# Six row buffers and loads five blocks ahead in the expert blocks of a two-layer recurrent kernel on one Trainium2 core

## The reference, cut to what matters

```python
residual = x
xn = _layernorm(x, ln_g, ln_b)
abel = jax.nn.gelu(xn @ aw1 + ab1, approximate=False) @ aw2 + ab2
nonabel = _rotate(_moe(xn, gate_w, gate_b, ew1, eb1, ew2, eb2), gens)
gate = jax.nn.sigmoid(jnp.concatenate([abel, nonabel], axis=-1) @ gc_w + gc_b)
return residual + abel * (1.0 - gate) + nonabel * gate
```

## Time and profile before

| what | us |
|---|---|
| median of three runs | 700.93 |
| lowest and highest of them | 700.16, 703.9 |
| the profiled execution | 701.6 |
| its span, from first to last instruction | 699.9 |

### The profile page before, as it was taken

How to read it: one execution, slowest core, us unless ns; L and a number is a source line. 1 busy time by engine, 2 the same in 40 slices (tenths; PEclk the granted TensorE clock), 3 DMA queues, 4 the chain that set the end, 5 groups by cost and what they waited for, 6 DMA issues and landing times.

```text
span 699.9 us, 19558 instructions
## 1 busy us (share of the span) xinstructions
PE 628.5 (90%) x6221; PEld 443.3 (63%) x6222; DVE 494.0 (71%) x1302; ACT 414.1 (59%) x1144; POOL 445.4 (64%) x652
## 2 busy tenths in 40 slices
PE   4788988886988898998899999998999999999993
PEld 3667767676877775775354455456999855555442
DVE  5678785568667716999488888885444488887884
ACT  2565433443444455776566777875444377878793
POOL 7675888889048889992122487843333258878782
PEclk9999999999999999997799999999999999999997
DMA  9995111144677731110000011100222201111110
GB/s 243 264 321 159 41 43 58 42 111 110 96 114 136 137 64 35 32 32 5 1 32 1 13 32 32 39 22 24 67 68 71 57 22 43 33 32 32 32 47 16
DMA packets 69466, 48.34 MB, mean 69 GB/s; under 512 B 8011, under 2 KB 63750, under 8 KB 69382
## 3 DMA queue, kind: packets, MB, share of 16 engines
q1 hardware_dynamic: 62332, 34.09, 19.3%
q0 software_dynamic: 6144, 12.63, 7.6%
q10 hardware_dynamic: 906, 0.55, 0.3%
HBM read 24.00 MB, written 23.24 MB: 67 GB/s over the span
## 4 chain that ended last, share of the span: by engine, by line
PE 49%; DVE 15%; POOL 13%; issue 9%; ACT 6%; DMA 5%; SPq 0%; DVEq 0%; POOLq 0%; ACTq 0%
PE bank L1753 12%; PE bank L1012 6%; PE bank L1733 6%; PE bank L1824 5%; PE bank L1833 5%; POOL yg_first L1056 4%; ACT pb L1898 3%; DVE nmx L2065 3%; DMA xg<-x_half 3%; POOL spacer L1051 3%; PE bank L579 2%; DMA y_half<-ys 1%; DVE turns L1392 1%; PE bank L1116 1%; POOL pool_xy L365 1%
## 5 line engine op out<-in xcount | busy, mean ns | idle before, releaser
L1898 ACT ACTIVATE pb<-bank,nmx 128x512 f32<-128x512 f32 x256 | 173.6, 692 | 64.7 <-DVE nmx L2065 64.5
L2065 DVE TENSOR_REDUCE nmx<-bank 128x2 f32<-128x1024 f32 x128 | 155.2, 1216 | 15.2 <-PE bank L1753 14.4
L1230 ACT ACTIVATE turns<-bank,cols 128x128 f32<-128x128 f32 x148 | 46.4, 364 | 57.1 <-PE bank L1116 56.3
L1665 POOL TENSOR_TENSOR vs<-vt_first,rz 128x256 f32<-128x256 f32 x64 | 39.5, 617 | 61.5 <-DVE rz L2041 60.8
L1733 PEld LDWEIGHTS bank<-pb,vs 128*32 128x32 f32 x2048 | 54.1, 110 | 37.4 <-issue 22.2
L1733 PE MATMUL bank<-pb,vs 128*32 128x128 f32 x2048 | 68.9, 275 | 2.0 <-POOL vs L1665 2.0
L382 POOL DMA_INDIRECT x_half<-pool_xy,slot x64 | 62.6, 977 | 10.6 <-issue 10.6
L1753 PE MATMUL bank<-qk 64*128 64x512 f32 x256 | 65.6, 622 | 1.6 <-ACT pb L1898 1.5
L1753 PE MATMUL bank<-qk_first 64*128 64x512 f32 x256 | 65.8, 632 | 1.2 <-ACT qk_first L1282 0.7
L1665 POOL TENSOR_TENSOR vs<-vt,rz 128x256 f32<-128x256 f32 x64 | 39.3, 617 | 39.0 <-DVE rz L2041 34.8
L1698 POOL COPY xn_all<-w 128x512 f32 x39 | 24.0, 616 | 47.6 <-PE bank L1824 47.6
(11 more groups left out here) (275 smaller groups left out, 1444.7 us busy)
## 6 DMA issues: line engine op xcount, KB each, us to landing
y_half<-ys SPq DMA_DIRECT2D x74, 64.5 KB, 2.7
x_half<-zero SPq DMA_DIRECT2D x2, 2368.0 KB, 17.1
xg<-x_half SPq DMA_DIRECT2D x74, 64.0 KB
x_sorted<-zero SPq DMA_DIRECT2D x1, 2496.0 KB, 18.7
xn_all<-x_sorted SPq DMA_DIRECT2D x39, 64.0 KB, 1.8
y_sorted<-xn_all SPq DMA_DIRECT2D x39, 64.0 KB, 1.6
x_all<-in_L_attn_x_dram SPq DMA_DIRECT2D x8, 256.0 KB, 6.3
w<-in_L_ffn_W_dram SPq DMA_DIRECT2D x1, 2048.0 KB, 11.3
```

The source lines that it names most:

```text
L1665: pool.tensor_tensor(vs[s][:, :, :], vt[bt % 2][:, n // 2 % TT, :, :].rearrange("p j d -> p (j d)") .unsqueeze(1).broadcast_to([P, 2, D]), ...
L1898: act.activation(pb[s + ab][:, :], psum[score_banks(k) + ab], ACT.Exp, bias=nmx[:, s + ab:s + ab + 1], scale=1.0, accum_out=zz[:, s + ab:s ...
L2065: dve.tensor_reduce(nmx[:, s:s + 2], banks[:, score_banks(k):score_banks(k) + 2, :], AX.X, ALU.max, negate=True).then_inc(n_mx, 1)
```

## The change

There are six row buffers in place of four; the two new ones are `cmask` and `bv_bc`. A load thus waits for the transposition of the block six earlier, and in step i SyncE issues the load of block i+5, still ahead of the store of block i-3. The load of block 4, the first into `cmask`, waits for the end of the first attention. SyncE no longer waits for stores; VectorE waits for the store of the block six earlier in `finish_block`, from block 6 on. Two semaphores go: `f_w`, which nothing used, and `f_og`, whose two waits count on `f_gg` instead.

```diff
-        NXG = 4
-        xg0 = [sbe(f"xg0{i}", [P, D]) for i in range(NXG)]
+        NXG = 6
+        xg0 = [sbe(f"xg0{i}", [P, D]) for i in range(NXG - 2)] + [cmask, bv_bc]
...
-        f_w = sem("f_w")
...
-        f_og = sem("f_og")
...
-                act.activation(og[:, :], gt[:, :], ACT.Copy, bias=0.5, scale=-0.5).then_inc(f_og, 1)
+                act.activation(og[:, :], gt[:, :], ACT.Copy, bias=0.5, scale=-0.5).then_inc(f_gg, 1)
...
-                act.wait_ge(f_og, bt + 1)
+                act.wait_ge(f_gg, 2 * bt + 1)
...
-                if k >= NB0 - LEAD:
+                if k >= NY:
                     dve.wait_ge(o_st[k % NY], 16 * (k // NY))
...
-                dve.wait_ge(f_gg, bt + 1)
+                dve.wait_ge(f_gg, 2 * bt + 2)
...
+                if k == NXG - 2:
+                    sp.wait_ge(a_os, B * TT + 2)
                 if k >= NXG:
                     sp.wait_ge(o_T, k - NXG + 1)
-                if k >= NY + LEAD:
-                    sp.wait_ge(o_st[(k - LEAD) % NY], 16 * ((k - LEAD) // NY))
```

## The result

The changed kernel takes 700.26 us (median of 20 runs, 697.58 to 702.55). The kernel before, run beside it, takes 702.43 us (20 runs, 699.68 to 706.06). The ratio is 0.9963, with a 95% interval of 0.9949 to 0.9978: 2.6 us faster (1.5 to 3.6), where the two medians differ by 2.2 us. The forecast was a gain of 4.4 us, or 0.63%. The sign is right and the size is too large; at 0.37% the change lies within the 0.5% that was counted as no change.

What follows compares the result with a forecast made beforehand. The prediction took the expert stage's first half, paced by late row loads, to bound the kernel. Loads five ahead gave 4.4 us and the other parts nothing: 700.93 - 4.4 = 696.5 us, range 693.2 to 700.3.

Steps and rivals of the forecast that it cites:

- The loads bound the pace: Expert stage, first half: late row loads, 3.88 us against three blocks of lead, set the pace, measured at 1.333 us a block.
- first item: Loads five blocks ahead: the pace over 29 first-half blocks falls from 1.333 to 1.18 us, saving 4.4 us.
- rival A: Expert stage: VectorE sets a floor of about 1.25 us a block, so the gain is 2.4, 698.5 us; chance 0.18.
- the step that let the second layer move as a whole: After the residual of batch 0: the stage and the second layer move as a whole, so all 4.4 us arrive.
- The stall: VectorE's 4.94 us weight copy beside GpSimd's four bias adds: stays and hits a later block, nothing gained or lost.
- VectorE's wait at no price: VectorE's store waits from block 6 on: met 3 us early, counted as 0, up to 2.9 us without idle time.
- D: Expert stage: VectorE stops for stores and TensorE behind it, 4.8 us slower, 705.8 us; chance 0.06.
- SyncE: SyncE's dropped store waits: part of the load waits already counted; it can issue load, store and next load in 0.95 us.
- the merged semaphore: Changes only the number to be waited for: nothing.
- the first load into the mask's memory: Load of block 4, waiting for the attention's end: goes no later than about 139.7, where the buffer count held it; nothing.
- What carries the gain on: GpSimd's gathers start at the first half's last store, so all 4.4 us reach the residual of batch 0, at 260.7.
- Rival C: TensorE, ahead and idle 5 to 6 us in 255 to 275, drops to half clock: 3 us lost, 699.5 us; chance 0.08.

Runs made afterwards that it cites:

- e6: Changed kernel with VectorE's store waits moved back to SyncE, six buffers and loads five ahead kept: 773.28 us in one run, against 710.87 for the kernel before.
- e5: Kernel before with only the store waits moved from SyncE to VectorE, four buffers and loads three ahead: ratio to the kernel before 0.9999 (0.9971 to 1.0027).
- e7: Changed kernel with VectorE's store wait repeated five times in every block from 6 on: ratio to the kernel before 0.9998 (0.9971 to 1.0025).
- e3: Changed kernel with seven more unread matmuls on TensorE, filling its idle time ahead of a down projection: ratio to the kernel before 0.9977 (0.9951 to 1.0003).
- e1: Kernel before, unchanged, profiled a second time: ratio 1.0002 (0.9979 to 1.0024).
- e16: Kernel before, unchanged, profiled again in the fourth group: ratio 0.9998 (0.9977 to 1.002).
- e13: Kernel before with three of GpSimd's four bias adds moved among the second half's scatters: ratio to the kernel before 0.9975 (0.9942 to 1.0007).
- e2: Changed kernel, unchanged, profiled a second time: ratio to the kernel before 0.9944 (0.9919 to 0.9968).
- e15: Changed kernel, unchanged, run again in the fourth group: ratio to the kernel before 0.9956 (0.993 to 0.9982).
- e14: Changed kernel with three of GpSimd's four bias adds moved among the second half's scatters: ratio to the kernel before 0.9893 (0.9855 to 0.9932).
- e4: Changed kernel with five row buffers and loads four blocks ahead: ratio to the kernel before 0.9954 (0.9927 to 0.9981).
- e11: Changed kernel, unchanged, run again in the third group: ratio to the kernel before 0.994 (0.9912 to 0.9968).

## Why the forecast was right, and where it was not

**The loads bound the pace: right.** The waits for row loads went from 7.7 us to none, and the pace from 1.333 to 1.20 us a block. e6 shows it from the other side. The 1.04 us a block that the prediction worked out from the Trainium skill's rule (DMA: Bandwidth & Descriptors, "Anatomy of one DMA"), by which nothing would have been gained, is not what the runs show. That section gives its fit for DMAs that GpSimd issues, and these loads are SyncE's, so the rule was applied beyond what it states.

**The size of the first item: the step that failed.** The forecast put the faster pace at 4.4 us. The 29 blocks give, in the same two pieces, 19.75 - (167.10 - 149.04) = 1.69 us for blocks 7 to 22 and 18.90 - (192.91 - 176.09) = 2.08 us for 25 to 39 (176.09 is the start of block 25's transposition): **3.8 us, not 4.4**. I took 1.18 us from three blocks. Behind the stall it held (1.18), but ahead of it the pace is 1.19 to 1.20 in three profiles, and with the short interval at half clock just behind the stall the average is 34.88 / 29 = 1.203. That is between the forecast and rival A's floor of 1.25, nearer to the forecast. What holds the pace is not VectorE, as A had it, but TensorE, busy for 97% of blocks 27 to 39. This accounts for 0.6 us of the 1.8 by which the forecast of 4.4 missed the 2.6 measured; the rest lies in the step that let the second layer move as a whole, or in scatter (last item below).

**The stall: "nothing gained or lost" was too simple.** Blocks 22 to 25 took 178.44 - 169.75 = 8.69 us before and 176.09 - 167.10 = 8.99 after, 0.3 us lost. The stall's end is set by GpSimd (174.08 before, 173.29 after), not by how far the blocks have come: of the 2.2 us by which block 22 came sooner, counted from the first transposition (30.34 to 28.11), block 25 kept 1.9. The rest of the -4.18 us at the first gather is no part of the sum: 0.42 us ahead of the stage and 0.55 in blocks 0 to 7 gained, 0.25 from block 39 to the gather lost, which is scatter by the repeated profiles. That the profile still hit its milestones of 197.3, 248.4 and 260.7 within 0.3 us is partly owed to that.

**VectorE's wait at no price (D): right, within what was measured.** No bias add waits for a store, e5 loses nothing by the wait, and e7's pace puts one at 0.01 us a block or less in the first half. Only e7's median leaves room for more: 0.8 us in all, or 1.4 by the ends of the two intervals.

**SyncE, the merged semaphore, the first load into the mask's memory: right.** No wait for them appears, and TensorE's row reads `cmask` and `bv_bc` at the same pace.

**What carries the gain on: right as far as batch 7**, the last row of the table ahead of the end. Rival C's mechanism came as described (7.13 us idle, 6.80 us at 0.50), and its price of 3 us did not: the milestones across it lose nothing, and filling it in e3 brought no time.

**Between batch 7 and the end** is what stays open. The forecast let the second layer move as a whole. In eight profiles the time from the residual to the end was 434.8 and 434.1 (before and e1), 431.8 (e16) and 430.8 (e13) with the old loads, 435.2, 435.2, 434.8 and 434.6 (after, e2, e15, e14) with the new ones: 2.1 us longer in the mean. These are the profiles of the first and fourth group and the first two, without e3 (436.1) and e4 (436.4). In the second and third group, without e6, the same time is 440.6 in the mean of two with old loads and 440.9 of five with new ones, so the 2.1 us don't repeat there. Part of the differences is the clock at the seam of the layers. There is a stretch at 0.50 there in every one, but its length differs. Stretches of e16 and of e15:

```profile
333.10:336.50 3.40, 2.92 (x21) 1.32 (x21) 2.44 (x11) 1.50 (x4) 0.74 (x1) 0.50 0.00 0
```

```profile
329.90:343.50 13.60, 12.27 (x70) 5.51 (x70) 5.29 (x15) 6.35 (x14) 1.01 (x1) 0.50 0.01 1
```

From the last batch's sum to the second layer's first maximum takes 6.97 us in e16 and 9.61 in e15, so 2.6 us went there: e15 is 2.98 us ahead of e16 at the residual and 0.02 at the end. The changed kernel's own profile has 10.2 us at 0.50 there, before's 17.10, the opposite way. Over all profiles of the two kernels the seam favours neither: 9.61, 9.61 and 6.97 us before (mean 8.7), 9.15, 7.22, 9.61 and 9.15 after (8.8).

The mean granted clock of every timed execution says the same. It gives the time at 0.50 as 2 x (1 - clock) x span: 35 us before against 41 for e2 in the first group, 32 against 42 for e15 in the fourth. The 6 and 10 us more are about the length of the new stretch near 262 (6.8 in e2, 10.2 in e15), and with that hole filled, in e3, it is 36. In the third group, where e11 has no such stretch, it is 38 against 40. (Only e7, at 46 against 41, has more without one in its profile.) So the changed kernel spends more time at half clock, but in the hole where TensorE is ahead. The measured 2.6 and pooled 3.2 us (2.4 to 3.9) against the 4.1 of the stage, itself from six profiles, may be no more than scatter; no run shows a place for the difference.

The range (693.2 to 700.3) holds the measured median by 0.04 us. Against the kernel before beside it, which was 1.5 us above the median that the forecast started from, the gain was 0.6 of the one forecast, or half by the medians. That the range still holds it by so little is luck.

## What to carry to other kernels

A queue of loads that is late by a fraction of a microsecond in each step shows as many short waits, and the lead that cures it is the time from the step that lets the load go to its landing, its place behind the other DMAs of the queue included, over the pace: 3.88 us over 1.2 is 3.2 steps, so four were nearly enough (two late loads) and five left none late. A wait that stands ahead of the loads on their queue has to move before the lead can grow; together the two gave 0.4%, the first alone nothing that shows and the second alone 9% slower, in a single run. When a few blocks set the price of a pace, read it on both sides of whatever interrupts them: the larger prize here, 0.7 and 0.9% in two groups for moving three bias adds of the changed kernel, stood in the rows as one copy of 4.94 us that I had passed as "stays".

## What the runs showed of the hardware

- One VectorE copy of 128x256 float32 within on-chip memory, 0.28 us alone, lasted until the end of four GpSimd additions without a break (4.92 us together; the copy took 4.0 to 5.7 us in fourteen profiles); beside a single addition it took 0.98 to 1.75 us in e13 and e14, and ScalarE's copy of the same data was not held (0.42 us).
- The same kernel had medians of 702, 704, 711, 715 and 703 us in five groups of runs, the 711 and the 715 on a chip of the same number, which is more than the change is worth; only ratios against runs beside it could be read.
- The granted clock was 0.50, that is 1.2 GHz, over 3.4 to 17.1 us at the seam of the two layers, for the same kernel in different executions, and up to 2.6 us of the time hung on it.
- In e6, with fewer DMAs under way, a store released its waiter 1.8 to 2.1 us after its issue in the rows shown, against a landing of 2.3 us at least and 2.7 in the median in the earlier trace rows.
- With loads never late, TensorE was busy for 13.71 of 14.15 us of the stage, 1.18 us for each block of 128 rows.
